# A feed-forward kernel's change from up to down projection, with the work of eight units put in another order

## The reference

```
x = x + attn(layernorm(x))      # attn: for each l, softmax over the 4 x 4 scores, over c = 512; it adds its own input
x = x + ffn(layernorm(x))
ffn:  g = x Wg^T;  u = x Wu^T;  h = silu(g) * u;  y = h Wd^T
      Wg, Wu: 3584 x 1024, Wd: 1024 x 3584; each weight = NF4_CODE[code] * absmax of its block of 64
```

## Time and profile before

| | us |
|---|---|
| median of 3 runs | 1683.72 |
| the runs | 1682.87, 1683.72, 1685.55 |
| the profiled execution, its own time | 1685.55 |
| its span, from the first to the last instruction | 1683.8 |
| TensorE busy | 1636.6 (97%) |
| VectorE busy | 1204.6 (72%) |
| ScalarE busy | 1029.8 (61%) |

### The profile page before, as it was taken

One profiled execution on the slowest core, in us unless ns is written; L12 is line 12 of the kernel. 1 busy time (PEld: TensorE's weight loads), 2 busy tenths in 40 slices (PEclk: granted clock), 3 DMA queues, 4 the chain that ended last, 5 costly groups with the idle time before them and its releaser, 6 DMA issues.

```text
span 1683.8 us, 20171 instructions
## 1 busy us (share of the span) xinstructions
PE 1636.6 (97%) x7888; PEld 790.5 (47%) x7888; DVE 1204.6 (72%) x1540; ACT 1029.8 (61%) x1118; POOL 57.6 (3%) x98
## 2 busy tenths in 40 slices
PE   5798999999999999999999999999899999999999
PEld 5774444444444444444444444444344444444444
DVE  7797886676857667676676857677777758577566
ACT  5667776767757666676767767778796626343000
POOL 3152000000000000000000000000000000000000
PEclk9999999999999999999999999999999999999999
DMA  6240232323314222331422323234665444343773
GB/s 266 88 179 22 71 118 74 139 94 113 135 60 156 90 105 97 116 138 53 160 94 94 131 82 138 87 138 142 239 235 185 166 149 173 124 173 124 249 255 125
DMA packets 76895, 226.39 MB, mean 134 GB/s; under 512 B 5248, under 2 KB 19968, under 8 KB 76288
## 3 DMA queue, kind: packets, MB, share of 16 engines
q1 hardware_dynamic: 76800, 225.10, 37.3%
HBM read 156.93 MB, written 68.16 MB: 134 GB/s over the span
## 4 chain that ended last, share of the span: by engine, by line
PE 92%; DVE 4%; ACT 1%; DMA 1%; issue 1%; POOL 0%; SPq 0%; DVEq 0%; ACTq 0%; POOLq 0%
PE ps L1537 20%; PE ps L1538 20%; PE ps L1539 20%; PE ps L1675 10%; PE ps L1677 10%; PE ps L1676 10%; PE ps L1507 2%; DVE stats L928 1%; DMA codes<-q_dram 1%; ACT codes L641 1%; PE ps L1516 1%; PE ps L1493 1%; DMA xa<-x_dram 0%; DVE xa L1132 0%; PE ps L1480 0%
## 5 line engine op out<-in xcount | busy, mean ns | idle before, releaser
L641 ACT ACTIVATE codes<-codes 128x1024 f32<-128x1024 f32 (+1 forms) x672 | 707.9, 1054 | 160.9 <-DMA codes<-q_dram 147.0
L1370 DVE SCALAR_TENSOR_TENSOR xb<-ps,y_back,xb 128x512 f32<-128x512 f32 x140 | 103.9, 749 | 74.5 <-PE ps L1677 71.2
L1537 PE MATMUL ps<-xa,wg 128*128 128x512 f16 x388 | 147.0, 379 | 1.1 <-issue 1.1
L1537 PE MATMUL ps<-xb,rw 128*128 128x512 f16 x388 | 147.1, 379 | 0.7 <-ACT gs L723 0.7
L1537 PE MATMUL ps<-xa,rw 128*128 128x512 f16 x388 | 147.6, 380 | 0.0
L1538 PE MATMUL ps<-xa,rw 128*128 128x512 f16 x388 | 147.6, 380 | 0.0
L1539 PE MATMUL ps<-xa,rw 128*128 128x512 f16 x388 | 147.5, 380 | 0.0
L1538 PE MATMUL ps<-xb,wg 128*128 128x512 f16 x388 | 147.1, 379 | 0.0
L1537 PE MATMUL ps<-xb,wg 128*128 128x512 f16 x388 | 147.1, 379 | 0.0
L1539 PE MATMUL ps<-xb,wg 128*128 128x512 f16 x388 | 147.1, 379 | 0.0
L1538 PE MATMUL ps<-xb,rw 128*128 128x512 f16 x388 | 147.1, 379 | 0.0
(11 more groups left out here) (278 smaller groups left out, 2923.2 us busy)
## 6 DMA issues: line engine op xcount, KB each, us to landing
codes<-q_dram SPq DMA_DIRECT2D x84, 512.0 KB, 4.6
absm<-a_dram SPq DMA_DIRECT2D x69, 512.0 KB, 3.7
h_dram<-rw SPq DMA_DIRECT2D x28, 1024.0 KB, 4.2
gs<-h_dram SPq DMA_DIRECT2D x21, 1344.0 KB, 5.9
h_dram<-rw SPq DMA_DIRECT2D x28, 768.0 KB, 4.6
rw<-h_dram SPq DMA_DIRECT2D x11, 896.0 KB, 5.8
rw<-x_dram SPq DMA_DIRECT2D x16, 512.0 KB, 11.1
xa<-a_dram SPq DMA_DIRECT2D x13, 512.0 KB, 5.3
```

The costliest lines, as they stand in the source:

```text
L641: fn(real, real if step else whole, ACT.Prelu, bias=at0, scale=slope, alpha=left).then_inc(bends_done, 1)
L1370: return v.scalar_tensor_tensor(out=dst, in0=ps[:, bank, :], scalar=y_back[:, 0:1], in1=dst, op0=ALU.mult, op1=ALU.add)
L1537: mm(dst, w_hi, x_hi, start=(start and kt == 0), stop=False, skip_group_check=True)
```

## The change

It puts part of the down part's first units in another order, and changes the order of SyncE's queue at some places further on.

- `h_slot`: units 0 to 3 use the two places in `xa`, units from 4 on the three others (before: units 0 to 5 and from 6 on).
- SyncE: the stores of slots 54 and 55 both stand in unit 2's step, ahead of the loads of units 4 and 5. `load_after(60)` comes ahead of the load of unit 3. In the step of unit 32 the load of unit 35's `h` comes ahead of the rows of units 33 to 35. A finished row is stored when all its four parts are done, not in two halves.
- ScalarE: `h_high` of slots 54 and 55 stands at the end of units 1 and 2, behind the last take, and the unit's bends stand between the takes. The bends of units 2 and 3 are 3 and 6, not 6 and 3.
- VectorE: `h_low(54)` and `h_sums(55)` stand ahead of unit 2, job 61 is in unit 2, with its scale and sums ahead of the unit's adds, and `h_low(55)` follows unit 2. Jobs 60 to 63 have scale and sums ahead of the adds of their unit.

```
-UNIT_OF_JOB = {1: 60, 3: 61, 4: 62, 5: 63, ...
+UNIT_OF_JOB = {1: 60, 2: 61, 4: 62, 5: 63, ...
-STEPS = (6, 3, 6, 3, 6, 6, 6, 4)
+STEPS = (6, 3, 3, 6, 6, 6, 6, 4)
@@ h_slot
-            if v < 6:
+            if v < 4:
                 return v % 2, 16 * (v // 2 + 1)
-            t = (v - 6) % 3
-            return 2 + t, (32 if t == 2 else 16) * ((v - 6) // 3 + 1)
+            t = (v - 4) % 3
+            return 2 + t, (32 if t == 2 else 16) * ((v - 4) // 3 + 1)
@@ load_h
-                elif v < 6:
+                elif v < 4:
                     sp.wait_ge(d3_done, v - 1)
-                elif v < 9:
+                elif v < 7:
                     sp.wait_ge(c12_done, seven(SLOTS - 1))
...
@@ store_out
-                for half in (1, 0):
-                    sp.wait_ge(final, 4 * u + 4 - half)
+                sp.wait_ge(final, 4 * u + 4)
+                for half in range(2):
@@ SyncE, for v in range(NV)
-                if v == 1:
-                    load_h(v + 2)
-                elif v in (2, 4):
-                    store_h(SLOTS - 3 + v // 2)
                 if v in UNIT_OF_JOB:
                     load_after(UNIT_OF_JOB[v])
-                if v in (0, 2, 3, 4, 5):
+                if v < 2:
                     load_h(v + 2)
-                elif v == 6:
-                    load_h(8)
-                    load_h(9)
+                elif v == 2:
+                    store_h(SLOTS - 2)
+                    store_h(SLOTS - 1)
+                    load_h(4)
+                    load_h(5)
+                elif v == 3:
+                    load_h(6)
+                elif v + 3 < NV:
+                    load_h(v + 3)
+                if v == NV - UNITS - 2:
+                    load_row(0)
                 elif v == NV - UNITS:
                     for u in range(1, 4):
                         load_row(u)
-                    load_h(v + 3)
-                elif 6 < v < NV - 3:
-                    load_h(v + 3)
-                if v == NV - UNITS - 2:
-                    load_row(0)
@@ ScalarE, units 0 to 7
-                    act.wait_ge(w_done, UP_JOBS + 4)
+                    act.wait_ge(w_done, UP_JOBS + 3)
...
                 take(b1, 3, t).then_inc(first1_done, 1)
-                if t in (1, 3):
-                    h_high(SLOTS - 2 + t // 2)
-                else:
-                    for k, step in now[:2]:
-                        bend(k, step)
+                for k, step in now[:2]:
+                    bend(k, step)
...
                 take(b7, 1, t).then_inc(first3_done, 1)
-                for k, step in now if t in (1, 3) else now[5:]:
+                for k, step in now[5:]:
                     bend(k, step)
+                if t in (1, 2):
+                    h_high(SLOTS - 3 + t)
@@ VectorE: the written-out order of units 0 to 7 becomes
+            def unit(t):
                 k = UNIT_OF_JOB.get(t)
-                if k is not None:
-                    weights_begin(k)
+                late = t in (UNITS - 2, UNITS - 1)
+                if k is not None and not late:
+                    scale_codes(k)
+                    sum_blocks(k)
                 add_c22(t)
+                if late:
+                    scale_codes(k)
+                    sum_blocks(k)
                 if k is not None:
                     weight_halves(k)
-                add_rest(t)
+                if t >= UNITS:
+                    add_rest(t)
+
+            unit(0)
+            h_sums(SLOTS - 2)
+            unit(1)
+            h_low(SLOTS - 2)
+            h_sums(SLOTS - 1)
+            unit(2)
+            h_low(SLOTS - 1)
+            for t in range(3, NV - UNITS):
+                unit(t)
```

More of the change, by code:

```diff
@@ L23 @@
 DOWN_JOBS = UP_JOBS + 4
-UNIT_OF_JOB = {1: 60, 3: 61, 4: 62, 5: 63, 6: 64, 7: 65, 9: 66, 10: 67, 11: 68, 12: 69, 13: 70, 14: 71,
+UNIT_OF_JOB = {1: 60, 2: 61, 4: 62, 5: 63, 6: 64, 7: 65, 9: 66, 10: 67, 11: 68, 12: 69, 13: 70, 14: 71,
                17: 72, 18: 73, 19: 74, 20: 75, 21: 76, 22: 77, 25: 78, 26: 79, 27: 80, 28: 81, 29: 82, 30: 83}
@@ L889, in _ @@
                 take(b1, 3, t).then_inc(first1_done, 1)
-                if t in (1, 3):
-                    h_high(SLOTS - 2 + t // 2)
-                else:
-                    for k, step in now[:2]:
-                        bend(k, step)
+                for k, step in now[:2]:
+                    bend(k, step)
                 act.wait_ge(d2_done, t + 1)
                 take(b1, 0, t).then_inc(first2_done, 1)
-                if t not in (1, 3):
-                    for k, step in now[2:4]:
-                        bend(k, step)
+                for k, step in now[2:4]:
+                    bend(k, step)
                 act.wait_ge(d4_done, t + 1)
@@ L902, in _ @@
                 take(b5, 2, t).then_inc(first4_done, 1)
-                if t not in (1, 3):
-                    for k, step in now[4:5]:
-                        bend(k, step)
+                for k, step in now[4:5]:
+                    bend(k, step)
                 act.wait_ge(d3_done, t + 1)
```

## The result

The changed kernel took 1701.61 us (median of 4 runs, 1700.26 to 1704.78) against 1684.63 us for the kernel before in the same session (1682.87 to 1685.69). The ratio is 1.0104, 95% interval 1.0087 to 1.0122: 1.0% slower, 17.0 us, where 17.3 were forecast and 1701.0 us predicted.

A forecast was written before the change was run, and what follows sets the result against it. TensorE, busy 97% of the span, bounds the kernel, so reordering only moves its pauses. 2.0 + 1.0 + 4.0 + 2.4 + 4.05 + 2.4 + 1.5 = 17.3 us takes the median from 1683.7 to 1701.0, range 1692 to 1706.

The forecast's parts named there:

- Part 1: Unit 2: earlier codes of job 62 remove the take's pause, 7.3 us free; a small wait near 1180 releases nothing needed soon.
- Part 2: Unit 2: TensorE waits for VectorE's first add instead, a 6.7 us pause against 4.68 before; +2.0 us net.
- Part 3: Unit 3: with h_high(55) behind unit 2's last take, TensorE waits for VectorE's first add; +1.0 us, no slow clock.
- rival D: Slower: the late-issued store of slot 54 frees the rings late for h_high(55); 2 us late give 1703, or 1705; chance 0.10.
- Part 4: Unit 4: its h waits for h_low(55) and queues behind slot 55's stores; +4.0 us, and +2.4 for the slow clock.
- Part 5: Units 4 to 8: no added cost; unit 5's first add is ready at 5.6 against 6.47, covered by 0.9 us.
- Part 6: Unit 33: its row, held behind unit 35's h, lands 8.8 us into the unit; +4.05 us pause, +2.4 for the clock.
- Part 7: The end: both halves of the last row go out together, one behind the other; +1.5 us.
- A: Unit 4: its load passes the stores, leaving a pause of 0.8 and no slow clock; 5.6 less, 1695.4; chance 0.10.
- C: Unit 33: its row lands early enough for a pause under 1.4 us; some 1696; chance 0.07.
- B: Units 4 and 33: the clock stays full behind the two new pauses of 4 us; 4.8 less, 1696.2; chance 0.08.
- E: Faster: VectorE's chain in unit 2 fits under TensorE's work and units 3 and 4 stay covered; 1677.9; chance 0.03.

The follow-up runs named there:

- e7: Kernel before, with only the loads behind job 60 moved ahead of the load of unit 3's h: 1676.66 us, ratio 0.9959.
- e11: Changed kernel, with the store of slot 54 ahead of the loads behind job 61 in SyncE's queue: 1703.15 us, ratio 1.0105.
- e4: Changed kernel, with h in the places of the kernel before and unit 4's load ahead of the store of slot 55: 1696.37 us, ratio 1.0070.
- e10: Changed kernel, with only unit 4's load of h moved ahead of the stores of slot 55 in SyncE's queue: 1700.24 us, ratio 1.0089.
- e1: Changed kernel, with the rows of units 33 to 35 loaded ahead of unit 35's h again: 1696.57 us, ratio 1.0074.
- e2: Changed kernel, with each finished row stored in two halves, the first as soon as it is done: 1701.96 us, ratio 1.0101.
- e3: Changed kernel, with VectorE's adds of unit 2 right behind h_low of slot 54, ahead of h_sums of slot 55 and job 61: 1703.08 us, ratio 1.0110.
- e6: Changed kernel, with VectorE's old order in units 0 to 7, slot 54's store early, old h places, unit 4's load ahead of slot 55's store: 1690.99 us.
- e5: Changed kernel, with VectorE's old order in units 0 to 7 and the store of slot 54 ahead of the loads behind job 61: 1699.12 us.

## Why the prediction was right, point by point

**Part 1, right on the price, wrong on a small wait.** The take's wait went, and e7 shows its full worth of 7.3 us when nothing else is in the way. But the codes of job 62 still came late for their first bend, and "releases nothing that TensorE needs soon" did not hold:

```profile
1180.31 1.06 ACT L640 ACTIVATE codes<-codes 128x1024 f32<-128x1024 int32 x1 [0.89 <-DMA codes<-q_dram]
1181.28 1.25 ACT L873 ACTIVATE xa<-ps,y_back 128x512 f32<-128x512 f32 x2
1182.42 1.91 ACT L753 ACTIVATE rw<-gs 128x2048 f16<-128x2048 f32 x1
```

The two takes ran back to back, and `h_high(54)` behind them began 1.29 us after unit 2's start at 1181.13, not 0.78.

**Part 2, right, 0.5 short.** The pause in unit 2 was 7.19, not 6.7. By the trace the 0.5 us are those of part 1: `h_high(54)`, then `h_low(54)`, then all behind it on VectorE came 0.5 us later against the unit's start. No run tests this alone. VectorE's block sums began at 1188.45, in a trace whose unit 2 began 0.3 us earlier; forecast was 1188.15, and the rest of the chain took the 5.6 us of the earlier trace rows:

```profile
1188.45 0.69 DVE L1215 TENSOR_TENSOR rw<-gs 128x512 f32<-128x512 f32 x1
...
1193.68 0.42 DVE L1011 TENSOR_TENSOR tmp<-tmp 128x256 f32<-128x256 f32 x1
```

**Part 3, a wait was missing from the sum.** 2.5 us, not 1.0. The missing term had been written down as rival D: the store of slot 54, held in the queue behind job 61, frees the ring late. Its estimate there had the ring free "just in time", at 1200.6; the store landed at 1202.18, since it went out at 1193.27 and took 8.9 us. It cost 1.5 us (e11).

**Part 4, right, 0.7 short.** The three transfers took 1216.12 - 1206.53 = 9.6 us, not 9.1, which is 0.5 of the 0.7. The formula that the prediction sets beside its sum, from the Trainium skill (DMA: Bandwidth & Descriptors, Anatomy of one DMA), gave 8.3; that section fits it to transfers issued by GpSimd, and these are SyncE's. The slow clock's 2.4 was met. e4 shows the whole of part 4 to be worth 7.4 us; e10 splits the pause in about two halves.

**Part 5, the cover was mis-sized.** "Covered by 0.9 us" was wrong, and unit 5 lost 0.7. I had put the last bend of job 63 at 1.85 us into unit 5, as if ScalarE's takes waited for TensorE alone; but two bends stand between the second and the third take. In the trace the last bend starts at 1229.91, ends 3.4 us into the unit (start 1227.59), and the scaling starts right behind it, at 1231.00. No run tests this one alone; the trace is the evidence:

```profile
1225.78 2.14 ACT L640 ACTIVATE codes<-codes 128x1024 f32<-128x1024 f32 x2
1227.83 0.67 ACT L873 ACTIVATE xb<-ps,y_back 128x512 f32<-128x512 f32 x1
1228.40 1.04 ACT L640 ACTIVATE codes<-codes 128x1024 f32<-128x1024 f32 x1
1229.34 0.68 ACT L873 ACTIVATE xb<-ps,y_back 128x512 f32<-128x512 f32 x1
1229.91 1.05 ACT L640 ACTIVATE codes<-codes 128x1024 f32<-128x1024 f32 x1
```

**Part 6, right.** The row landed 9.2 us into unit 33 (VectorE's first add of it starts at 1606.11 after waiting for `xb<-x_dram`; forecast 8.8). The pause was 4.41 (4.05), the clock 1.69 (2.4), the sum 6.1 for 6.45, so a pause too short and a clock cost too high cancelled in part. e1 confirms the cause.

**Part 7, right.** 1.3 for 1.5; e2 gives it back.

The misses of parts 2 to 5 (3.4 us too low) and of parts 6 and 7 (0.6 too high) would have made the forecast of the median 1703.8. The profiled execution, forecast at 1702.9 us, took 1703.5 for the span and 1.8 around it, 1705.3.

That the median of the runs came to 1701.6, within 0.6 us of the forecast, is in part luck. Less the 1.75 us around the span and a down part of 540.5 it leaves 1159.3 us for the first part, and the shortest first part in any trace was 1160.4. For the other kernels here the same sum leaves 1160.1 to 1163.7. So the timed runs of the changed kernel were some 2 us faster than its own trace and the others' first parts account for. What was shorter in them no trace shows. It is also why e1, e4 and e10 gained 5.0, 5.2 and 1.4 us by medians and 6.4, 7.4 and 3.2 in the down part. The mechanism is shown by the traces and the experiments; the close number is not further evidence for it.

**The rivals.** A and C fell, with one load that waited its turn and a row that landed late. B fell: each pause of over 4 us had its slow clock (before, had shown only one such pause, of 4.68 us, not several). D was true in part, beside the main case. E fell at its first point: the first add of unit 2 came 7.2 us too late. F fell: the interval of the ratio, 1.0087 to 1.0122, is clear of 1.

## What to carry to other kernels

In a kernel whose engines all run in written-out order, the pauses form a chain, and the profile names only the one that comes last: taking away the largest wait of the changed kernel (e3) moved it to the next unit and gained nothing, while a single moved issue in the kernel before (e7) gained all 7.3 us, since everything behind it was in time. Price a reordering by following each queue to the instruction that the bounding engine waits for, SyncE's too: an issue that waits holds up each transfer behind it, and five of the costs here were, wholly or in part, a transfer behind a wait that was not its own: unit 2 of the kernel before, 1.5 of the 2.5 us in unit 3, about half of unit 4's pause, unit 33, and the two pauses of e6.

## What the hardware showed that was not expected

A slow clock behind a pause cost TensorE 1.5 to 2.6 us in the down part, and no more for a longer pause: 2.5 behind 7.2 us, 1.7 behind 10.3 us (e3), 2.0 behind 13.1 us (e5), 1.5 behind 2.5 us (e10). Pauses of 1.8 and 2.3 us (e6) had none. For the long pauses much of the slow stretch lies in the pause itself and costs nothing: in e5 the granted clock was 0.50 from about 1204 to 1217.5, and TensorE was idle until 1213.5 of it.

The same instructions ahead of the down part took from 1160.4 to 1165.5 us in the profiled executions, with the edits all behind them. For the kernel before, such a range can hold the whole spread of its runs (1682.35 to 1687.05 us over all sessions); for the changed kernel it can't, since its runs with the down part of the trace would leave 1158.0 to 1162.5. No kernel was profiled twice, so how its down part varies from run to run is open.
